# Dividing the attention output instead of the exponentials, and a new order of the steps

## The reference

```python
sc = softmax(where(damb, scores, NEG)) * smb * damb
distcum, disttot = cumsum(sc), sum(sc)
dist = sqrt(clip((disttot - distcum) * pos, 0))      # pos = |i - j|
te = clip(exp(dist * gamma), 1e-05, 100000.0)
scores = softmax(where(damb & smb, scores * te, NEG))
if zero_pad: scores[:, :, 0, :] = 0.0                # layer 2 alone
out = einsum('bhqk,bhkd->bhqd', scores, v)
x = layernorm(query + out @ oW.T + ob)
# layers 0 and 2 also: x = layernorm(x + relu(x @ w1.T + b1) @ w2.T + b2)
```

## Time and profile before

| | us |
|---|---|
| median of the runs | 3467.85 |
| profiled execution, whole | 3470.1 |
| its span, first to last instruction | 3468.2 |
| DVE busy | 3088.9 (89%) |
| PE busy | 2920.0 (84%) |
| ACT busy | 2773.3 (80%) |
| POOL busy | 457.4 (13%) |
| transfers, share of 16 engines' time | 10.2% |

### The profile page before, as it was taken

How to read it: one execution, slowest core, us unless ns; L and a number is a source line. 1 busy time by engine, 2 the same in 40 slices (tenths; PEclk the granted TensorE clock), 3 DMA queues, 4 the chain that set the end, 5 groups by cost and what they waited for, 6 DMA issues and landing times. The chain is left out here.

```text
span 3468.2 us, 66824 instructions
## 1 busy us (share of the span) xinstructions
PE 2920.0 (84%) x19008; PEld 2144.3 (62%) x19008; DVE 3088.9 (89%) x5665; ACT 2773.3 (80%) x10276; POOL 457.4 (13%) x599
## 2 busy tenths in 40 slices
PE   1788888988888988888988888988888988888986
PEld 1566665666665666665666665666665666665664
DVE  3789999999999999999999999999999999999994
ACT  2688888888888888888888888888888888888883
POOL 1111111111111111111111111111111111111110
PEclk9799999999999999999999999999999999999997
DMA  5000111100111000111100110010110100111000
GB/s 154 22 27 17 30 32 28 30 26 16 29 32 28 29 27 15 30 32 28 29 26 16 30 32 28 27 29 15 30 32 28 28 27 16 30 32 28 26 20 10
DMA packets 166403, 101.63 MB, mean 29 GB/s; under 512 B 36696, under 2 KB 165708, under 8 KB 166220
## 3 DMA queue, kind: packets, MB, share of 16 engines
q1 hardware_dynamic: 166220, 99.97, 10.2%
HBM read 56.26 MB, written 10.01 MB: 19 GB/s over the span
## 5 line engine op out<-in xcount | busy, mean ns | idle before, releaser
L775 ACT ACTIVATE X<-X,nm 128x128 f32<-128x128 f32 x1536 | 594.7, 395 | 103.7 <-DVE nm L907 100.7
L775 ACT ACTIVATE E<-scores_ps,nm 128x128 f32<-128x128 f32 x1536 | 545.0, 405 | 82.8 <-DVE nm L876 82.8
L1027 POOL TENSOR_SCALAR_AFFINE_SELECT X<-X 128x1024 f32<-128x1024 f32 x192 | 212.2, 1105 | 2252.9 <-DVE X L901 2252.9
L601 PE MATMUL gen_ps<-f_buf,up_w 128*128 128x256 f32 x2048 | 486.7, 389 | 0.8 <-ACT f_buf L437 0.8
L891 DVE SCALAR_TENSOR_TENSOR X<-suffix,rz,decay 128x128 f32<-128x128 f32 x1536 | 420.4, 346 | 58.6 <-PE gen_ps L651 32.3
L728 PE MATMUL gen_ps<-down_w,hidden 128*128 128x256 f32 x2048 | 460.2, 379 | 0.5 <-ACT hidden L467 0.4
L876 DVE TENSOR_REDUCE nm<-scores_ps 128x8 f32<-128x1024 f32 x320 | 389.5, 1217 | 51.5 <-PE scores_ps L630 34.5
L601 PEld LDWEIGHTS gen_ps<-f_buf,up_w 128*128 128x128 f32 x2048 | 390.5, 196 | 71.8 <-issue 17.8
L885 DVE TENSOR_TENSOR_SCAN suffix<-chain,E 128x1024 f32<-128x1024 bf16 x192 | 434.3, 2262 | 0.0
L728 PEld LDWEIGHTS gen_ps<-down_w,hidden 128*128 128x128 f32 x2048 | 381.5, 190 | 56.7 <-ACT hidden L467 1.3
L651 PE MATMUL gen_ps<-ident,X 128*128 128x128 f32 x2560 | 350.9, 281 | 66.6 <-DVE X L928 64.2
(11 more groups left out here) (122 smaller groups left out, 5097.2 us busy)
## 6 DMA issues: line engine op xcount, KB each, us to landing
k_diag<-k_f SPq DMA_DIRECT2D x768, 32.0 KB, 1.9
xk_diag<-xk_f SPq DMA_DIRECT2D x1024, 8.0 KB, 1.7
ctx_f<-in_ctxT SPq DMA_DIRECT2D x32, 256.0 KB, 2.8
x_f<-in_xT SPq DMA_DIRECT2D x32, 256.0 KB, 3.3
x_t<-in_x SPq DMA_DIRECT2D x32, 256.0 KB, 3.5
ctx_t<-in_ctx SPq DMA_DIRECT2D x32, 256.0 KB, 3.3
cx_f<-in_ctxT SPq DMA_DIRECT2D x32, 256.0 KB, 2.8
out<-out_t SPq DMA_DIRECT2D x32, 256.0 KB, 2.2
```

What stands on the lines that cost most here:

```text
L601: mm = nc.tensor.matmul(ps[:, i * T:(i + 1) * T], w[:, k, c * P:(c + 1) * P], src[:, k, :], start=(k == 0), stop=(k == C - 1))
L775: a = nc.scalar.activation(dst[:, cols], src[:, cols], ACT.Exp, bias=minus_max[:, h:h + 1], accum_out=sums[:, h:h + 1])
```

## The change

What it does:

- **Late division.** `prob` is gone. `pt` turns the exponentials as `exp2` (in a cross unit `exp1`) left them. A new step `widen` on POOL spreads the unit's 8 reciprocals over 128 columns, 16 or 32 to a head (two 128x128 operations for a layer unit, one for a cross unit), and takes over the factor `keep_row`. `att` on PE first turns these blocks (two, or one) into the free half of its own PSUM bank. A new step `spread` on ACT copies them to `att_f` or `xatt_f`, and the copy of the attention output becomes a product with them, always on DVE.
- **Distance.** `dist` is now the reciprocal and the scan, which works in place in `E` with three slots instead of two plus `suffix`; a new step `x` holds the 8 products. On ACT `effect` becomes three steps, `ln`, `root` and `effect`, and other work stands between them.
- **Banks** come from the table `BANKS`.
- **Sums.** The residual sum is two operations of 128x256, one for each sequence, with a semaphore for each, as are the statistics.
- **Tables.** All five tables are new. DVE's copies were vx, att (1,1), att (3,1,1), k 2, v 2, kx and four `pt` halves, and are now all ten att products, k 1, k 2, v 1, v 2, kx and six `pt` halves; vx goes to ACT.

```diff
-TENSOR = [(2, ("up", 2, 0)), (2, ("up", 2, 2)), (2, ("up", 2, 3)), (2, ("up", 2, 1)), (1, ("pt", (0, 0), 0)),
...
+TENSOR = [(1, ("up", 0, 2)), (1, ("up", 0, 3)), (0, ("k", 0)), (1, ("down", 0)), (2, ("att", (3, 0, 0))),
...
+BANKS = [3, 0, 2, 1, 0, 1, 2, 3, 2, 1, 2, 3, 1, 0, 3, 2, 3, 1, 0, 2, 3, 2, 0, 1, 3, 2, 3, 2, 0, 1, 3, 0, 2, 2, 1, 0,
+    3, 2, 1, 0, 3, 1, 2, 3, 2, 1, 0, 3, 1, 2, 0, 1, 0, 3, 1, 2, 0, 2]
...
-E_SLOTS = 2
+E_SLOTS = 3
...
             elif kind == "att":
                 u = step[1]
-                if is_layer(u):
-                    last = copy(att_f[u[0] % 2][:, u[1], :, :].rearrange("p c s -> p (c s)"), ps[:, 0:C * S])
-                else:
-                    last = copy(xatt_f[:, u[1], u[2], :], ps[:, 0:S])
+                dst, n = att_of(u)
+                eng.wait_ge(spread_done, spread_order.upto(now, d, ("spread", u)))
+                last = nc.vector.tensor_tensor(dst, ps[:, 0:n], dst, ALU.mult)
...
             def probs_turn(ps, now, d, u, half):
 
-                pe.wait_ge(norm_done, prob_order.upto(now, d, ("prob", u)))
+                exponentials_done(pe, now, d, u)
...
                 in_sbuf(now, d, ("att", u), value_step, ("pt", u, 0), ("pt", u, 1))
+                pe.wait_ge(wide_done, wide_order.upto(now, d, ("widen", u)))
+                for c in range(C if is_layer(u) else 1):
+                    first = (C if is_layer(u) else 1) + c
+                    nc.tensor.transpose(ps[:, first * S:(first + 1) * S], rz_wide[:, W_SLOT[u], c * P:(c + 1) * P], ident[:, :])
...
+            def logarithm(now, d, u):
+                x = X[:, X_SLOT[u], :]
+                act.wait_ge(x_done, x_order.upto(now, d, ("x", u)))
+                nc.scalar.activation(x, x, ACT.Ln, bias=root_floor[:, :]).then_inc(ln_done, 1)
...
+            def spread(now, d, u):
+                ps, _ = take(act, now, d, ("att", u))
+                dst, n = att_of(u)
+                nc.scalar.copy(dst, ps[:, n:2 * n]).then_inc(spread_done, 1)
...
+            def later_keys(now, d, u):
+
+                dve.wait_ge(exp1_done, exp1_order.upto(now, d, ("exp1", u)))
+                nc.vector.reciprocal(rz1[:, UNIT[u], :], z1[:, UNIT[u], :]).then_inc(scan_done, 1)
+                e = E[:, E_SLOT[u], UW - 1::-1]
+                nc.vector.tensor_tensor_scan(e, chain[FIRST_KEY_MASK[u[0]]][:, ::-1], e, 0.0, ALU.mult, ALU.add
+                                             ).then_inc(scan_done, 1)
...
-            def normalise(now, d, u):
-
-                dve.wait_ge(rz2_done, recip_order.upto(now, d, ("recip", u)))
-                x = unit_heads(X[:, X_SLOT[u], :])
-                nc.vector.tensor_tensor(x, x, rz2[:, UNIT[u], :].unsqueeze(2).to_broadcast([P, UH, S]), ALU.mult
-                                        ).then_inc(norm_done, 1)
...
-                nc.vector.tensor_tensor(res[:, i, :, :], ps[:, :].rearrange("p (b d) -> p b d", b=G),
-                                        residual(l, which)[:, :, :], ALU.add).then_inc(free, 1)
-                read_out(dve, now, d, step)
                 for b in range(G):
-                    ins = nc.vector.bn_stats(stats[:, i, b, :], res[:, i, b, :])
-                ins.then_inc(stats_done, 1)
...
+                    nc.vector.tensor_tensor(res[:, i, b, :], ps[:, b * D:(b + 1) * D], residual(l, which)[:, b, :], ALU.add
+                                            ).then_inc((res_done, free)[b], 1)
...
+            def widen(now, d, u):
+
+                back, (_, last) = wide_order.last(("widen", u), W_SLOTS)
+                i = GEN_BANK["att", last]
+                wait_apart(pool, gen_full[i], gen_order[i].upto(now, d, ("att", last), back))
+                wait_apart(pool, rz2_done, recip_order.upto(now, d, ("recip", u)))
+                rz = rz2[:, UNIT[u], :]
+                if is_layer(u):
+                    for c in range(C):
+                        heads = rz.rearrange("p (k c j) -> p c k j", k=2, c=C)[:, c, :, :]
+                        dst = rz_wide[:, W_SLOT[u], c * P:(c + 1) * P].rearrange("p (k j d) -> p k j d", k=2, j=2)
+                        ins = nc.gpsimd.tensor_scalar(dst, heads.unsqueeze(3).to_broadcast([P, 2, 2, DK]),
+                                                      keep_row[:, 0:1] if u[0] == 2 else 1.0, None, ALU.mult)
```

More of the change, by code:

```diff
@@ L199 @@
     assert len(slots) % n == 0
-assert len(dist_order.events) % X_SLOTS == 0 and len(xexp_order.events) % XX_SLOTS == 0
+assert len(x_order.events) % X_SLOTS == 0 and len(xexp_order.events) % XX_SLOTS == 0
+W_SLOTS = 2
+W_SLOT = {step[1]: i % W_SLOTS for i, (_, step) in enumerate(wide_order.events)}
 UNIT = {u: i for i, u in enumerate(SLOT)}
@@ L301, in build @@
         xk_diag = sb("xk_diag", [P, 2, BANK])
[L302 to L303 removed]
+        E = sb("E", [P, E_SLOTS, UW + 1])
         X = sb("X", [P, X_SLOTS + XX_SLOTS, UW])
@@ L812, in turn_of @@
                     else:
-                        {"exp1": exp1, "effect": effect, "exp2": exp2}[step[0]](now, d, step[1])
+                        {"exp1": exp1, "ln": logarithm, "root": root, "effect": effect, "exp2": exp2, "spread": spread}[step[0]](now, d, step[1])
             run_turns(act, turn_of)
@@ L980, in turn_of @@
                     else:
-                        {"max1": max1, "dist": distance, "scores2": scores2, "max2": max2, "recip": recip,
-                         "prob": normalise}[step[0]](now, d, step[1])
+                        {"max1": max1, "dist": later_keys, "x": distance, "scores2": scores2, "max2": max2, "recip": recip}[step[0]](now, d, step[1])
             run_turns(dve, turn_of)
@@ L1038, in turn_of @@
                 for g, d, step in now.steps(POOL):
-                    {"select": select, "dev": deviation}[step[0]](now, d, *step[1:])
+                    {"select": select, "dev": deviation, "widen": widen}[step[0]](now, d, *step[1:])
             run_turns(pool, turn_of)
```

168 lines of the change are left out of this document (86 added, 82 removed), and 55 rows, old and new, of tables (SCALAR, TENSOR, VECTOR).

## The result

| | median us (lowest to highest) | ratio to before, 95% interval |
|---|---|---|
| before | 3467.43 (3464.98 to 3469.31) | |
| after | 3373.01 (3372.31 to 3374.74) | 0.9729 (0.9712 to 0.9746) |

What follows compares the result with a forecast made beforehand. DVE bounded before (92%); afterwards PE, DVE and ACT nearly level, waits deciding. DVE 88.9 + 9.1 or PE 91.6 + 6.4 made 98.0 us a turn, 31 x 5.5 = 170 saved: 3297 us, own range 3251 to 3359, 8-in-10 3200 to 3410.

Steps and rivals of the forecast that it cites:

- Attention output priced as a copy: DVE's product of attention output with spread reciprocals costs what a copy does, 0.33 or 0.20 us each, +2.25 a turn.
- Two `tok` pairs a turn held by a select: DVE's `tok` meets POOL's select twice a turn, (2,1) and (2,2), not three times: -0.8 us.
- `widen` on POOL holds DVE by 1.5 us a turn: 16 new POOL operations a turn hold DVE by +1.5 us, ends 0 and +4.9; seven meet two-input work.
- Sixteen turned blocks, 1.75 us of PE: PE turns 16 more blocks a turn, priced from `pt` blocks at +1.75 us, giving 91.6 us.
- Residual sums in halves, 0 with ends of -1 and +1: DVE's six residual sums a turn, each split in two, change its load by 0 us, ends -1 and +1.
- The wait ahead of `turn` (2,1), 0.6 us: PE's wait for layer 2's normed tokens falls from 4.92 us to 0.6.
- `o` 2 waits 1 to 2 us: On PE, `o` 2 waits 1 to 2 us for spread, effect, `scores2` and product, 2.9 us, beside `v` 0.
- Rivals 3 and 4: Hand-over through ACT and DVE before `o`: eats half the gain, 3409 us, chance 0.09; or slower, 3521 us, 0.09.
- Rival 2: All 16 of POOL's widens hold DVE, +4.9 us: 100.1 us a turn, 3362 us, chance 0.12.
- Rivals 1 and 5: DVE still bounds with fewer waits, 3204 us, chance 0.16; or no effect, DVE's saving becomes idle, 3468 us, 0.04.
- Where they wait: Layout of the new order's waits: PE's idle time falls from 13.6 to 6 to 8 us, DVE's rises to about 9.
- 89.9 + 8.1: Second reading of the 98.0 us turn: PE's work with no slow stretch left, 89.9 us, plus 8.1 idle.

Runs made afterwards that it cites:

- e3: The kernel after with each block of `rz_wide` turned twice by PE, 16 more blocks a turn: 3387.85 us.
- e10: The kernel after with the residual sum as one operation of 128x512 again, the statistics keeping their two semaphores: 3390.70 us.
- e2: The kernel after without `widen`, turned blocks and spread, the product made a plain copy, outputs not divided: 3351.55 us.
- e5: The kernel after with one idle 128x1024 DVE reduction a turn added behind `max1` (1,1), in the short stretch: 3414.42 us.
- e6: The kernel after with one idle 128x1024 DVE reduction a turn added behind `max1` (3,1,1), in the long stretch: 3374.25 us.
- e4: The kernel after with `tok` (2,2) put ahead of `scores2` (1,1) in DVE's table: 3323.82 us.

## Why the prediction was right or wrong

**The loads were near.** DVE has 87.0 us a turn against 88.9 forecast, PE 92.5 against 91.6, ACT 84.7 against 85. The first two lie a little outside what the prediction asked for (88 to 90 and 90 to 92), the turn, 100.7, further (97 to 99). The groups of DVE that answer to the earlier trace rows:

```profile
L929 DVE SCALAR_TENSOR_TENSOR X<-E,rz,decay 128x128 f32<-128x128 f32 x1536 | 431.0, 350 | 3.7 <-DVE E L920 0.5 <-issue 0.4
L991 DVE SCALAR_TENSOR_TENSOR x_tok<-res,rstd,norm_b 128x256 f32<-128x256 f32 x128 | 81.9, 681 | 21.7 <-POOL rstd L1078 21.7
L991 DVE SCALAR_TENSOR_TENSOR a_tok<-res,rstd,norm_b 128x256 f32<-128x256 f32 x128 | 81.8, 680 | 2.4 <-POOL rstd L1078 2.4
L455 DVE TENSOR_TENSOR att_f<-gen_ps,att_f 128x256 f32<-128x256 f32 x192 | 76.8, 413 | 21.0 <-ACT att_f L842 21.0
L455 DVE TENSOR_TENSOR xatt_f<-gen_ps,xatt_f 128x128 f32<-128x128 f32 x128 | 33.0, 276 | 7.9 <-ACT xatt_f L842 7.9
L991 DVE SCALAR_TENSOR_TENSOR y_tok<-res,rstd,norm_b 128x256 f32<-128x256 f32 x64 | 27.4, 466 | 0.0
```

- *Attention output priced as a copy:* right, 0.41 and 0.28 us.
- *Two `tok` pairs a turn held by a select:* right; `y_tok` is at its bare 0.47, `a_tok` and `x_tok` at 0.68.
- *`widen` on POOL holds DVE by 1.5 us a turn:* the count of seven operations beside the products of `x` was right. One was priced at 0.305 us and takes 0.53 to 0.66 where nothing holds it. Wrong was that it holds DVE for its length: the 48 products a turn went from 420.4 to 431.0 us in the whole kernel, 0.33 us a turn, or 0.05 for each of the seven. This explains 1.2 of the 1.9 us by which DVE's load came out lower.
- *Sixteen turned blocks, 1.75 us of PE:* too low. It holds for a block behind another, as in e3, but the blocks come in twos and ones. A pair takes 0.36 us from its start to that of the next matmul, as below, and a single one 0.20; six pairs and four single ones are 3.0 us a turn.

```profile
1010.41 0.44 PE L684 MATMUL gen_ps<-ident,rz_wide 128*128 128x128 f32 x2
1010.78 0.64 PE L690 MATMUL gen_ps<-probs_f,v_t 128*32 128x128 f32 x16
```

- *Residual sums in halves, 0 with ends of -1 and +1:* the value is -0.57 us a turn (e10), inside the ends but not 0, and as latency, not load.
- *The wait ahead of `turn` (2,1), 0.6 us:* near, 0.84. *`o` 2 waits 1 to 2 us:* wrong, all `o` steps together wait 5.6 us in the whole kernel.
- *Rivals 3 and 4, the hand-over:* the waits at the `o` steps did not come. The whole price of the division, with its load, is 0.7 us a turn net (e2).
- *Rival 2, the widens hold DVE:* its 100.1 us a turn and 3362 us are the nearest of all to what was measured, by luck: of the 4.9 us that it charged, 0.33 came.
- *Rivals 1 and 5* are out by their numbers, 3204 and 3468 us.

**The step that was mis-sized is "Where they wait", in its last line: PE's idle time falls to 6 to 8 us and DVE's rises to about 9.** The sum took PE as 91.6 + 6.4, which measured 92.5 + 8.25, and DVE as 88.9 + 9.1, which measured 87.0 + 13.7. I had seen that DVE reaches `tok` (2,2) late and that this leaves "up to 5 us of idle PE", and yet took an idle time near the low end of my range, since the loads seemed to leave room. There are three errors in it. First, I took a mean over the turn: PE at 91.6 of 98.0 looks possible, but PE waits for DVE in the short stretch, in which DVE has no room; what e5 and e6 show of it is said above. Second, the slow clock did not go with the wait ahead of (2,1). The reading 89.9 + 8.1 dropped it, while 91.6 + 6.4 kept its 1.7 us; it moved with the largest wait to (2,2) and costs 1.7 us a turn there. Third, PE's work at full clock rose by 2.7 us a turn (88.1 to 90.8) and not by 1.75, the turned blocks above; this is why 92.5 came and not 91.6. e4 takes the slow clock and a part of the idle time away with one exchange and lands at 3323.82, which is 27 us from the forecast; so the kernel could do most of what the sum said, but the order as given did not.

The turn itself was read as 103.5 us from two starts of one instruction; over ten turns it is 104.1, since it alternates. With it the forecast would have been a larger saving still, so this error partly hid the other: 100.7 - 98.0 = 2.7 us a turn was missed, and 0.6 of it was made good by chance. The 29 turns of the loop miss 2.1 us each, 61 us of the 76; most of the rest is that the forecast counted the filling and draining as saving like two turns more, and together they saved nothing.
